# Two of four expert mixtures of input blocks three and four, moved from VectorE to ScalarE and GpSimd

## What is computed

```python
x = x + 0.5 * ffn(layernorm(x), router_weight, router_bias, expert_bias)
x = x + attn(layernorm(x), Wq, Wk, Wv, Wo, Wg, Win, dt_bias, A_log_bias, gnorm_w)
x = x + 0.5 * ffn(layernorm(x), router_weight, router_bias, expert_bias)

def ffn(flat, ...):                       # 64 experts, the top 8 of each token
    scores = softmax(flat @ router_weight.T + router_bias)
    topk_w, topk_idx = top_k(scores, 8)
    w_dense = scatter of topk_w at topk_idx
    return flat * topk_w.sum(-1) + w_dense @ expert_bias

def attn(x, ...):                         # 32 heads of 128, 8 key heads, chunks of 128 tokens
    q, k, v = rope(x @ Wq.T), rope(x @ Wk.T), x @ Wv.T
    dt = softplus(x @ Win.T + dt_bias); g = -dt * exp(A_log_bias); G = cumsum(g) in a chunk
    y = (scores * decay) @ (v * dt) + (q * exp(G)) @ state      # state carried over 16 chunks
    return (rmsnorm(y) * gnorm_w * silu(x @ Wg.T)) @ Wo.T
```

## Time and profile before

| | us |
|---|---|
| median of 3 runs | 1623.02 (1622.58 to 1623.47) |
| the profiled execution | 1621.97 |
| its span, first to last instruction | 1620.1 |
| busy: TensorE | 1581.5 (98%) |
| VectorE | 1295.7 (80%) |
| ScalarE | 1091.8 (67%) |
| GpSimd | 1234.5 (76%) |
| mean granted TensorE clock | 0.992 of full speed |

### The profile page before, as it was taken

The page is one execution under the profiler, slowest core; times in us unless marked ns, Lnnn a source line. Parts: engine busy times, 40 slices in busy tenths (PEclk is TensorE's granted clock), DMA queues, the critical chain, the costliest instruction groups (busy, mean ns, idle before and its releaser), DMA issues.

```text
span 1620.1 us, 33715 instructions
## 1 busy us (share of the span) xinstructions
PE 1581.5 (98%) x11028; PEld 883.4 (55%) x11028; DVE 1295.7 (80%) x2945; ACT 1091.8 (67%) x2987; POOL 1234.5 (76%) x1191
## 2 busy tenths in 40 slices
PE   7899999999999999999999999999999999999986
PEld 5555555555555555555555555555555555555554
DVE  7988788877878788787878778787878778788877
ACT  5667667766766677666767677666677667676653
POOL 5767787877877788777878788777888778777764
PEclk8999999999999999999999999999999999999998
DMA  6045467544665457454664446564565546753422
GB/s 231 29 83 97 77 109 108 87 90 66 119 102 101 75 95 114 86 98 74 103 111 93 80 79 115 93 102 70 112 105 88 90 66 120 101 88 75 76 48 105
DMA packets 322711, 152.34 MB, mean 94 GB/s; under 512 B 174313, under 2 KB 305897, under 8 KB 321513
## 3 DMA queue, kind: packets, MB, share of 16 engines
q1 hardware_dynamic: 322536, 150.18, 51.7%
HBM read 103.48 MB, written 38.01 MB: 87 GB/s over the span
## 4 chain that ended last, share of the span: by engine, by line
PE 89%; DVE 3%; POOL 3%; issue 2%; ACT 1%; DMA 1%; SPq 0%; ACTq 0%; POOLq 0%; DVEq 0%
PE B L330 28%; PE B L332 28%; PE B L331 28%; PE B L586 1%; DMA KD<-K 1%; DVE BS L492 1%; DVE ACC L734 1%; POOL ACC L703 0%; PE B L916 0%; PE B L915 0%; PE B L920 0%; POOL RR L1497 0%; PE B L987 0%; PE B L992 0%; PE B L986 0%
## 5 line engine op out<-in xcount | busy, mean ns | idle before, releaser
L1451 POOL TENSOR_TENSOR QS<-QS,SIN 128x512 f32<-128x512 f32 x160 | 212.6, 1329 | 112.3 <-ACT QS L1175 112.3
L330 PE MATMUL B<-WH,XTH 128*128 128x128 bf16 (+1 forms) x992 | 269.3, 296 | 0.7 <-DVE QF L1650 0.7
L331 PE MATMUL B<-WL,XTH 128*128 128x128 bf16 (+1 forms) x992 | 269.3, 296 | 0.0
L332 PE MATMUL B<-WH,XTL 128*128 128x128 bf16 (+1 forms) x992 | 269.3, 296 | 0.0
L330 PE MATMUL B<-XTH,WH 128*128 128x512 bf16 x640 | 243.3, 380 | 1.0 <-DVE G L1670 1.0
L332 PE MATMUL B<-XTH,WL 128*128 128x512 bf16 x640 | 243.2, 380 | 0.0
L331 PE MATMUL B<-XTL,WH 128*128 128x512 bf16 x640 | 243.2, 380 | 0.0
L1174 ACT ACTIVATE QS<-B 64x512 f32<-64x512 f32 x160 | 95.1, 595 | 194.3 <-PE B L332 187.0
L1490 POOL TENSOR_TENSOR ZS<-YF,ZS 128x512 bf16<-128x512 f32 x128 | 153.5, 1199 | 94.9 <-ACT ZS L1248 94.9
L1729 DVE SCALAR_TENSOR_TENSOR YF<-B,RR,G 128x128 f32<-128x128 f32 x512 | 144.2, 344 | 93.9 <-POOL RR L1497 93.6
L1486 POOL TENSOR_TENSOR PL<-PF,PH 128x512 bf16<-128x512 f32 x128 | 148.2, 1158 | 60.7 <-ACT PH L1216 60.7
(11 more groups left out here) (210 smaller groups left out, 4202.9 us busy)
## 6 DMA issues: line engine op xcount, KB each, us to landing
masked_dram<-rows_store SPq DMA_DIRECT2D x126, 258.0 KB
ROWS<-masked_dram SPq DMA_DIRECT2D x126, 256.0 KB, 2.9
STAGE<-in_wall SPq DMA_DIRECT2D x108, 256.0 KB, 2.8
ACC<-in_x SPq DMA_DIRECT2D x3, 1024.0 KB, 8.8
out<-ACC SPq DMA_DIRECT2D x3, 1024.0 KB, 3.9
ZT<-ZS SPq DMA_TRANSPOSE x128, 5.6
ACC<-in_x SPq DMA_DIRECT2D x4, 256.0 KB, 3.6
COS<-in_cos SPq DMA_DIRECT2D x1, 1024.0 KB, 13.2
```

The source lines that it names most:

```text
L330: nc.tensor.matmul(out_, ah, bh, start=first, stop=False)
L331: nc.tensor.matmul(out_, ah, bl, start=False, stop=False)
L332: return nc.tensor.matmul(out_, al, bh, start=False, stop=last)
L1451: nc.gpsimd.tensor_tensor(QS[:, sl, :], QS[:, sl, :], SIN[:, t0:t0 + TB], ALU.mult).then_inc(sin_ready.sem, 1)
```

## The change

For blocks three and four (f = 2 and 3), chunks 0 and 1 stay as they are. For chunks 2 and 3, ScalarE reads the bank, scales it by HRC and writes it to FIRST.XT, whose turned input the logits have consumed by then (`act_half`); GpSimd adds it to the chunk (`pool_half`). Those who waited for VectorE's addition now wait for one of the two: the statistics for GpSimd's (h_added), the next user of the bank for ScalarE's (h_part). The counts of f_acc are shifted by what VectorE no longer does. The calls are put into the written-out orders of ScalarE, GpSimd and VectorE.

```diff
--- before.py
+++ after.py
@@ -184,10 +184,19 @@
             return f in (NB + 1, NB + 2)
 
         def mixed_by_dve(f):
-            return (0, 1) if shared(f) else range(BLK)
+            return (0, 1) if shared(f) or f in (2, 3) else range(BLK)
+
+        def split_mix(f):
+            return f in (2, 3)
 
         def acc_at(f, i):
-            return f_acc.at(f, i) - 2 * max(0, f - NB - 1)
+            return f_acc.at(f, i) - 2 * max(0, f - NB - 1) - 2 * max(0, min(f, NB) - 2)
+
+        def wait_mixed(engine, f, i):
+            if split_mix(f) and i >= 2:
+                engine.wait_ge(h_added.sem, 2 * (f - 2) + i - 1)
+            else:
+                engine.wait_ge(f_acc.sem, acc_at(f, i))
 
         def part(f, i):
             return FINAL.XT[:, 0, i if f == NB + 1 else i - 2, :]
@@ -300,6 +309,7 @@
         f_wt, f_wtc, f_mix, f_acc = (Sem(n, k) for n, k in (("f_wt", 1), ("f_wtc", 1), ("f_mix", 4), ("f_acc", 4)))
         f_tp2, f_xth, f_xtl = (Sem(n, 4) for n in ("f_tp2", "f_xth", "f_xtl"))
         f_part, f_added = Sem("f_part"), Sem("f_added")
+        h_part, h_added = Sem("h_part"), Sem("h_added")
         r_sums, r_centred = Sem("r_sums"), Sem("r_centred")
 
 
@@ -486,7 +496,7 @@
                 if w == 0 and f == 0:
                     dve.wait_ge(x0_landed[i].sem, 16)
                 if w == 1:
-                    dve.wait_ge(f_acc.sem, f_acc.at(f, i))
+                    wait_mixed(dve, f, i)
                 if f >= NB:
                     dve.wait_ge(out_free.sem, out_free.at(KVH - 1, (f - NB) * BLK + i))
                 nc.vector.bn_stats(BS[:, w, f % 2, i, :], A[:, i, :]).then_inc(f_bs[w].sem, 1)
@@ -674,7 +684,10 @@
                 elif f > NB:
                     pe.wait_ge(f_acc.sem, acc_at(f - 1, i))
                 elif f < NB and (f or i >= 2):
-                    pe.wait_ge(f_acc.sem, f_acc.at(f, i - 2))
+                    if i < 2 and split_mix(f - 1):
+                        pe.wait_ge(h_part.sem, 2 * (f - 3) + i + 1)
+                    else:
+                        pe.wait_ge(f_acc.sem, acc_at(*((f, i - 2) if i >= 2 else (f - 1, i + 2))))
                 nc.tensor.matmul(mix(f, i)[:, :], expert(f).WT[:, i, :], expert(f).EBH[:, :], start=True, stop=False)
                 nc.tensor.matmul(mix(f, i)[:, :], expert(f).WT[:, i, :], expert(f).EBL[:, :], start=False, stop=True).then_inc(f_mix.sem, 1)
 
@@ -708,6 +721,20 @@
             act.wait_ge(f_lg.sem, f_lg.at(NB + 2, 0))
             act.wait_ge(f_mix.sem, f_mix.at(f, i))
             nc.scalar.activation(part(f, i), mix(f, i)[:, :], ACT.Copy, scale=FINAL.HRC[:, f % NB, i:i + 1]).then_inc(f_part.sem, 1)
+
+        def act_half(act, f, i):
+            act.wait_ge(f_hrc.sem, f_hrc.at(f, 0))
+            act.wait_ge(f_lg.sem, f_lg.at(f, 0))
+            act.wait_ge(f_mix.sem, f_mix.at(f, i))
+            nc.scalar.activation(FIRST.XT[:, f % 2, i, :], mix(f, i)[:, :], ACT.Copy,
+                                 scale=FIRST.HRC[:, f % NB, i:i + 1]).then_inc(h_part.sem, 1)
+
+        def pool_half(pool, f):
+            A = chunks_of(f)
+            for i in (2, 3):
+                pool.wait_ge(f_res.sem, f_res.at(f, i))
+                pool.wait_ge(h_part.sem, 2 * (f - 2) + i - 1)
+                nc.gpsimd.tensor_tensor(A[:, i, :], A[:, i, :], FIRST.XT[:, f % 2, i, :], ALU.add).then_inc(h_added.sem, 1)
 
         def pool_added(pool, f, chunks):
             A = chunks_of(f)
@@ -840,7 +867,7 @@
 
             pe.wait_ge(d_g.sem, d_g.at(f // 2, 0))
             if f == 0:
-                pe.wait_ge(f_acc.sem, f_acc.at(NB - 1, BLK - 1))
+                pe.wait_ge(h_part.sem, 4)
                 pe.wait_ge(c_landed.sem, 16 * 6)
             else:
                 pe.wait_ge(d_rows.sem, d_rows.at(f - 1, 0))
@@ -1291,9 +1318,11 @@
             act_normalise(act, 1, (1,))
             act_turned(act, 3, (3,))
             act_normalise(act, 1, (2,))
+            act_half(act, 2, 2)
             split_hi(0, 7)
             swap(0, 0, 0, 0)
             act_turned2(act, 1, (1,))
+            act_half(act, 2, 3)
             act_exp(act, 3)
             split_hi(0, 8)
             act_normalise(act, 1, (3,))
@@ -1303,6 +1332,8 @@
             act_turned2(act, 1, (3,))
             swap(0, 0, 2, 2)
             swap(0, 0, 3, 3)
+            act_half(act, 3, 2)
+            act_half(act, 3, 3)
             act_normalise(act, 2, (0,))
             hi(0, 0, 0)
             act_normalise(act, 2, (1,))
@@ -1534,11 +1565,13 @@
             pool.wait_ge(rope_landed.sem, 32)
             times_sin(0, 0, 0)
             split_lo(0, 5)
+            pool_half(pool, 2)
             pool_scales(pool, 3)
             times_sin(0, 0, 1)
             pool_residual(pool, 3)
             times_sin(0, 0, 2)
             pool_rstd(pool, 1, 2)
+            pool_half(pool, 3)
             split_lo(0, 8)
             split_lo(0, 7)
             times_sin(0, 0, 3)
@@ -1789,9 +1822,7 @@
             dve_mixed(dve, 2, (1,))
             dve_stats(dve, 1, 2, (0, 1))
             times_cos(0, 0, 0, 0)
-            dve_mixed(dve, 2, (2,))
             dve_logits(dve, 3)
-            dve_mixed(dve, 2, (3,))
             dve_stats(dve, 1, 2, (2,))
             dve_choose(dve, 3)
             dve_stats(dve, 1, 2, (3,))
@@ -1807,7 +1838,6 @@
             dve_dt_abs(dve, 0)
             add_sin(0, 0, 1, 1)
             add_sin(0, 0, 2, 2)
-            dve_mixed(dve, 3, (2, 3))
             times_cos(0, 0, 3, 3)
             dve_stats(dve, 1, 3, (2, 3))
             dve_series(dve, 0, 0)
```

## The result

The change makes the kernel slower. The median of six runs is 1627.85 us (1626.81 to 1631.50), beside 1622.79 us (1621.72 to 1623.47) of the kernel before in the same six rounds; the ratio is 1.0035, with a 95% interval of 1.0022 to 1.0048, so 3.6 to 7.8 us. The profiled execution took 1627.62 us (span 1625.8, mean granted clock 0.990), 5.65 more than the one before. The prediction was 1628.2 in a range of 1623.8 to 1630.4.

A forecast was written before the change was run, and what follows sets the result against it. The loop runs at TensorE's pace and the chain from the first sums has no slack, so an opening delay reaches the end whole: 1623.0 + 3.5 (queues) + 1.7 (clock) = 1628.2 us, range 1623.8 to 1630.4.

The forecast's parts named there:

- Block three: Opening, chunk 2: cosine product +1.0 us waiting for the swap, statistics and everything behind them 0.87 us later.
- Block four and piece 7: GpSimd's queue: block four's additions delay the splits of pieces 8 and 7 to 75.65, +3.7 us.
- The wait that ends last: Before TensorE's last turn: piece 9's load, split and ScalarE's copies hold VectorE's XTL, +3.5 us; VectorE's own work off path.
- the second rival: Piece 9's load not last; VectorE's wait for the additions delays the series, +2.4, 1625.4; chance 0.15 together with no effect.
- The clock: TensorE's stall before the last turn grows to about 4.1 us and its clock falls to 1.2 GHz, costing 1.7 us.
- The rival in which the clock holds: TensorE's clock doesn't fall behind the stall; only the queue's shift is left, +3.5, 1626.5; chance 0.17.
- The sum: Whole kernel: queue delay 3.5 plus clock 1.7, +5.2 us, giving a median of 1628.2.
- The two terms: The queue delay of +3.5 us up to TensorE's turn and the 1.7 us for TensorE's clock behind it.
- The rival of contention: First series: GpSimd holds two VectorE instructions for 0.9 each, adding up to 1.8, 1630.0; chance 0.10.
- The faster case: Opening: new work fits idle time of ScalarE and GpSimd, VectorE's 2.65 us come off, 1620.4; chance 0.10.

The follow-up runs named there:

- piece 7 first: Changed kernel with GpSimd's split of piece 7 moved ahead of block four's two additions, the split of piece 8 staying behind them; ratio 1.0026.
- both cures: Changed kernel with GpSimd's split of piece 7 ahead of block four's additions and nine unread matmuls in TensorE's stall; ratio 1.0010.
- the stall filled: Changed kernel with 16 unread matmuls put into TensorE's stall ahead of block three's last turn; ratio 1.0017.
- block four only: Kernel before with only block four's two additions moved off VectorE, block three's staying there; ratio 1.0029.
- the series spread: Changed kernel with the second series of dt spread over the first four steps of the loop; ratio 1.0063.
- block three placed otherwise: Kernel before with only block three moved: ScalarE's swap ahead of the scalings, GpSimd's additions right behind the residual; ratio 1.0001.

## Why the prediction was right

- **Block three.** Forecast: +1.0 on the cosine product, +0.87 on the statistics. Measured net: +1.0 and +1.0. The wait of 0.94 is for the swap, as worked out. "Everything behind it is 0.87 later" was not right: with the fall of the clock at 61.7, which the prediction doesn't have, it is 1.5 at the next cosine products, and 1.2 at the additions of the sine products, since L828 took 0.41 in place of 0.73.
- **Block four and piece 7.** Forecast: additions from 70.9, splits done at 75.65, issue 75.7. Measured: 71.53, 76.38 and 76.40, net +4.2 in place of +3.7. Of the 0.5, 0.4 lies ahead of the additions (71.30 net), where swap 3 came 0.35 later than forecast (those additions are 1.2 late in place of 0.87), so that GpSimd waited 0.96 for the scaling in place of 0.3; the rest is in the splits, 2.37 long in place of 2.28.
- **The wait that ends last.** Forecast: the load of piece 9, the split and the copy, not VectorE. The chain names exactly these; XTL is 3.9 late net in place of 3.5. Putting piece 7 first left VectorE's queue as the wait that ends last, at 2.3: the second rival, with 2.4 for its price, was the right next in line, and it is what is left of the loss after both cures (+2.0). With the order on GpSimd left as it is, VectorE's queue stands at 2.9.
- **The clock.** Forecast: it falls, 1.7 us. It fell; the price was 2.1 by the kernel with the stall filled. The term was mis-sized because the length was taken from the earlier trace rows, 3.5 us at 0.53; here the low stretch began inside the stall and still covered some 4.7 us behind the turn. The rival in which the clock holds is out; with the clock held by the unread matmuls the loop is at +3.7, beside its 3.5.
- **The sum.** Forecast +5.2; measured +5.8 net in the loop, +5.7 by the ratio. The two terms were each short by 0.4, which makes +6.0 at the first sums; that the loop is at 5.8 is the last point below.
- **The rival of contention** was forecast at the first series. There it came (L843 0.70, L844 1.35), but the series had 0.7 us to spare before XTL, so it cost nothing as long as the reload came last. Two L812 rows of 0.9 were its price; L843 and L844 together were held for 1.3. It came again at the second series, which the prediction did not price.
- **A step that came out right for a reason that was not given.** The prediction shifts everything behind the first sums by the same amount, with the consumer of KD at 110. It is at 108.4. From the first sums to KD the way of the earlier trace rows is 2.8 us shorter after (+6.0 became +3.2), nearly all of it in two DMAs: the rows' store took 1.6 in place of 2.8, the turning of the keys 8.7 in place of 10.1. Then TensorE waits for VectorE and behind it, 0.93, 0.89 and 0.35 (the timeline above, 129.72 to 137.58), and the loop is at +5.8 again. VectorE is late there since its second series starts 5.0 late, net, and is held for 1.8 more. Why the two DMAs were shorter is not shown; the turning of the keys took between 8.6 and 10.8 us over the twelve kernels. That the loop's delay equals that of the first sums is thus the sum of two effects that the prediction doesn't have, and luck; with piece 7 first, where the series took 3.68, the KD step and the loop are both at +3.6.

The faster case failed at the point that the prediction gave for it: the additions had to end before VectorE reached the statistics, and ended 1.3 and 1.5 us after. Better placing (block three) removes these waits, but then VectorE is slowed by GpSimd, so also that version gains nothing.

## What to carry to other kernels

Moving work off a busy engine pays only if the work ends, on its new engines, before the old one would have started on what follows; and what stands behind the moved work in the new queue is part of its price. Here the wait that ended last was for a reload, released by a split two places further back in GpSimd's queue, on a path that has nothing to do with VectorE: look for such releases of DMAs first, and put them ahead. But take only the distance to the next wait in line for their price: of the 3.9 us at the turn the reload's was at most 1.0, and 2.3 were left when it and the contention were gone. Where a wait on TensorE grows, read the granted clock behind it as well, for the fall adds to the wait; and where a fall vanishes, look at what the engines now do at the same time before the gain is booked. Where a DMA stands on the path, compare its length in the traces first: here one and the same DMA differed by up to 2.2 us, as much as the effects looked for.

## What the runs showed of the hardware

- **Where the clock falls.** Stalls of 1.46 and 1.84 us ahead of the turn, of 1.49 to 1.70 ahead of block four's weights and of 2.04 to 2.19 ahead of the matmuls on KD left it at 2.4 GHz. Those of 2.55 ahead of the weights, 2.26, 3.12, 3.88, 3.93 and 3.98 ahead of the turn, and 3.51 ahead of KD were followed by a granted clock of 0.50. The length of one stall doesn't decide alone: ahead of the fall at 100.2 before stood stalls of 1.65, 0.26 and 1.05 close together, and ahead of the 2.26 one of 0.68.
- **What a fall costs.** In the changed kernel the clock stayed low until about 85.5 us, though TensorE had worked without a gap since 82.2. The low stretch behind the start of the turn was 5.7 us with block four only, 4.7 after, 4.4 after with the series spread and 2.8 with piece 7 first; the fall cost 2.6, 2.2, 2.0 and 1.2 us between the turn and the first sums, a little under half of each.
- **VectorE beside GpSimd.** An instruction with two SBUF inputs of 128x256 takes 0.42 us alone and 1.20 beside back-to-back GpSimd instructions; six chained ones take 2.73 or 4.51. In the kernel with block three placed otherwise, L624 started at 58.89, GpSimd's split ended at 59.80, and L624 ended 0.29 later. The Trainium skill, SBUF — State Buffer, section "SBUF: two separate sides", tells of an exclusive lock for a whole instruction: with that the rows agree, and the 1.8 more of the series are two instructions of the six, 1.38 and 1.26 long after in place of 0.42, each of which ended 0.28 behind the GpSimd instruction that it ran beside.
- **The same DMA.** The turning of the keys took 8.6 to 10.8 us over the twelve kernels, the rows' store 1.6 to 2.8.
